# An attention phase with POOL summing the probabilities, two units in one product run, and the maxima of two heads in the two halves of the array

## What is computed

```python
o1 = attn(q, k1, v1, causal)            # branch 0: all keys, causal; values of rank 32
o2 = attn(q, ks, vs)                    # branch 1: 256 selected keys
o3 = attn(q, kw, vw, window of 64)      # branch 2: local window, causal
o = g[:, 0] * o1 + g[:, 1] * o2 + g[:, 2] * o3
return o @ Wproj                        # softmax over keys in each branch, scale 1/8
```

## Time and profile before

| | us |
|---|---|
| median of 3 runs | 2779.24 (2778.72 to 2779.59) |
| the profiled execution, its own time | 2781.34 |
| its span | 2779.4 |
| first and last product L1344 | 706.2 and 2379.5 |

### The profile page before, as it was taken

The page is one execution under the profiler, slowest core; times in us unless marked ns, Lnnn a source line. Parts: engine busy times, 40 slices in busy tenths (PEclk is TensorE's granted clock), DMA queues, the critical chain, the costliest instruction groups (busy, mean ns, idle before and its releaser), DMA issues. The chain is left out here.

```text
span 2779.4 us, 45396 instructions
## 1 busy us (share of the span) xinstructions
PE 2320.6 (83%) x16656; PEld 1545.5 (56%) x16656; DVE 1628.3 (59%) x3043; ACT 1266.2 (46%) x2777; POOL 669.8 (24%) x687
## 2 busy tenths in 40 slices
PE   5585858663999999999999999999999999601995
PEld 3464545442666666666666666566566666401884
DVE  4758575734466466466566576566565564450766
ACT  2354545440455555555455455555555555310442
POOL 0265656573011011011011011011010010145332
PEclk9697978765999999999999999999999999655997
DMA  2255555479547646556655565664664660611113
GB/s 97 97 219 184 216 187 201 172 269 226 126 93 146 132 101 139 122 118 131 127 121 122 120 136 114 136 129 104 137 137 96 138 130 10 158 39 47 48 53 110
DMA packets 222841, 360.53 MB, mean 130 GB/s; under 512 B 68794, under 2 KB 124701, under 8 KB 222240
## 3 DMA queue, kind: packets, MB, share of 16 engines
q1 hardware_dynamic: 216288, 348.43, 50.1%
q0 software_dynamic: 4320, 8.43, 0.9%
q10 hardware_dynamic: 2016, 0.77, 0.2%
HBM read 229.58 MB, written 126.56 MB: 128 GB/s over the span
## 5 line engine op out<-in xcount | busy, mean ns | idle before, releaser
L1370 ACT ACTIVATE prob<-ps 128x512 f32<-128x512 f32 (+5 forms) x1600 | 637.8, 441 | 665.8 <-PE ps L1325 656.3
L1434 DVE TENSOR_REDUCE maxima<-ps 128x1 f32<-128x512 f32 (+3 forms) x768 | 387.5, 547 | 291.4 <-PE ps L1250 147.0
L1344 PE MATMUL ps<-prob,plain 128*32 128x512 f32 (+5 forms) x3200 | 512.0, 443 | 0.0
L1400 POOL TENSOR_TENSOR products<-products,sums 128x256 f32<-128x256 f32 x192 | 140.8, 733 | 1540.3 <-DVE sums L1425 1539.0
L1439 DVE TENSOR_REDUCE maxima<-ps 128x2 f32<-128x512 f32 (+1 forms) x512 | 293.7, 606 | 192.6 <-PE ps L1261 98.4
L1425 DVE RECIPROCAL sums<-sums 128x256 f32<-128x256 f32 x192 | 331.9, 1736 | 97.6 <-ACT sums L1383 97.6
L1317 PE MATMUL ps<-q1a_s,k1a_s 128*128 128x512 f32 (+3 forms) x768 | 303.0, 395 | 0.0
L1325 PE MATMUL ps<-q1b_s,k1b_s 128*128 128x512 f32 (+3 forms) x768 | 301.1, 393 | 0.0
L1344 PE MATMUL ps<-prob,v_s 128*32 128x512 f32 (+3 forms) x1536 | 284.3, 491 | 0.0
L1250 PE MATMUL ps<-k1a_s,q1a_s 128*128 128x512 f32 (+3 forms) x768 | 234.5, 374 | 0.5 <-DVE maxima L1439 0.2
L1381 ACT ACTIVATE products<-ps,gates_a 64x512 f32<-64x512 f32 x192 | 131.0, 682 | 196.4 <-PE ps L1344 196.3
(11 more groups left out here) (333 smaller groups left out, 4889.8 us busy)
## 6 DMA issues: line engine op xcount, KB each, us to landing
qh_dram<-pairs SPq DMA_DIRECT2D x96, 512.0 KB, 2.7
kwh_dram<-pairs SPq DMA_DIRECT2D x64, 512.0 KB, 2.7
qa_s<-qh_dram SPq DMA_DIRECT2D x128, 256.0 KB, 4.7
kwa_s<-kwh_dram SPq DMA_DIRECT2D x128, 256.0 KB, 7.7
q1a_s<-qh_dram SPq DMA_DIRECT2D x128, 256.0 KB, 4.8
qb_s<-qh_dram SPq DMA_DIRECT2D x64, 256.0 KB, 9.3
kwb_s<-kwh_dram SPq DMA_DIRECT2D x64, 256.0 KB, 10.3
k1a_s<-k1ah_dram SPq DMA_DIRECT2D x32, 512.0 KB, 6.9
```

What stands on the lines that cost most here:

```text
L1344: mm = pe.matmul(ps[at:at + VD, SCORES + k % 2, q0 - c * CH:q0 - c * CH + w], w_, m.prob[:, n % PROBS, h, 0:w], start=first, stop=True, sk ...
L1370: act.activation(m.prob[:, u % PROBS, h, 0:w], ps[:, turn % SCORES, 0:w], ACT.Exp, scale=SCALE).then_inc(s["exp_done"], 1)
L1400: pool.tensor_tensor(o, o, m.sums[:, br, cc], ALU.mult).then_inc(s["divided"], 1)
L1434: ins = dve.tensor_reduce(partial[:, h, i, part:part + 1], bank[:, 0:w], AX, ALU.max)
```

## The change

- The products of branches 0 and 1 leave out the ones. Two units of the same width, one of branch 0's second half and one of a short list (branch 1, then branch 0's first half), are multiplied by their values in one run: two heads of each unit, in the four column tiles.
- POOL sums the probabilities of these 16 units into `acc`, in 12 additions and one copy a side. Two "total" steps a side multiply `acc` by the ones, in a fill bank; ACT copies them out ("take"). Branch 2 keeps its ones.
- The units stand in another order: the 9 of branch 2 first, then the 16 in pairs. `prob` holds 6 units.
- The queries are laid out so that the high parts of head 0 lie in partitions 0 to 63 and those of head 1 in 64 to 127. A maxima step takes both heads, each in 64 rows of the array (row tiles of 64 by 128), in two banks at once. There are 20 such steps a side, still with 3 fill banks and 40 reductions by DVE.
- `qb`, `kwb`, `ksb`, `vw` and `vs` are in one buffer instead of two, and have loads of their own, which wait until the side before has used them.
- The reciprocals and divisions of branch 0 stand at the beginning of the next side, both halves; those of branch 1 follow its total, in the last third of an odd side.

```diff
-SUMS = [(1, 0), (2, 0), (1, 1), (2, 1), (0, 0), (0, 1)]
-UNITS = units()
+def groups():
+
+
+    found = units()
+    sets = [found[2, c][i:i + 2] for c in range(NC) for i in range(0, len(found[2, c]), 2)]
+    short = found[1, 0] + found[1, 1] + found[0, 0]
+    return sets + [list(x) for x in zip(short, found[0, 1])]
+
+
+UNITS = sum(groups(), [])
+TOGETHER = [tuple(UNITS.index(x) for x in group) for group in groups()]
 LAST = [max(u for u, x in enumerate(UNITS) if x[:2] == k) for k in SUMS]
...
+OCCUPANTS = [-2, 0, 1, 2, 3, 1]
...
+def summing():
+
+
+    found, released, former = [], {}, {}
+    for u, (br, c, j, q0, w) in enumerate(UNITS):
+        if br == 2:
+            continue
+        if (br, c) not in former:
+            former[br, c] = u
+            continue
+        released[u] = len(found) + 1
+        if former[br, c] is not None:
+            released[former[br, c]] = len(found) + 1
+        found.append((u, br, c, former[br, c], q0 - c * CH, w))
+        former[br, c] = None
+    return found, released
+
+
+SUMMING, RELEASED = summing()
...
-PROBS = 4
+PROBS = 6
...
-    max0 = [("max0", side, h, i, part) for h in range(HP) for i in range(NT) for part in range(1 + (i >= NT // 2))]
-    max1, max2 = [[(kind, side, h, k) for h in range(HP) for k in range(NT // 2)] for kind in ("max1", "max2")]
-    todo = max2 + max1[:3] + [("rows", side, 2)] + max1[3:] + max0[:3] + [("rows", side, 1)] + max0[3:]
+    max0 = [("max0", side, i, part) for i in range(NT) for part in range(1 + (i >= NT // 2))]
+    max1, max2 = [[(kind, side, k) for k in range(NT // 2)] for kind in ("max1", "max2")]
+    todo = max2 + max1[:2] + [("rows", side, 2)] + max1[2:] + max0[:2] + [("rows", side, 1)] + max0[2:]
...
-    if w % 2 == 0 and w > 0:
-        pieces = [("divide", w - 1, len(SUMS) - 1, piece) for piece in range(PIECES)] + [("proj", w - 1, 1)]
+    if w > 0:
+        pieces = closing(w - 1)
-        ready = range(u - 2, u) if u >= 2 and u % 2 == 0 else range(u - 1, u) if u == len(UNITS) else ()
-        for done in ready:
-            todo.append(("products", w, done))
-        for done in ready:
-            if done in LAST:
-                k = LAST.index(done)
-                todo.append(("sum", w, k))
-                if w % 2 == 1 and (k < len(SUMS) - 1 or w == SIDES - 1):
-                    pieces += [("divide", w, k, piece) for piece in range(PIECES)]
-                    if SUMS[k][0] == 0:
-                        pieces.append(("proj", w, SUMS[k][1]))
+            todo += [("acc", w, op) for op, x in enumerate(SUMMING) if x[0] == u]
+        ready = [group for group, follower in zip(TOGETHER, TOGETHER[1:] + [(len(UNITS),)]) if follower[0] == u]
+        for group in ready:
+            todo.append(("products", w, group))
+            for done in sorted(LAST.index(x) for x in group if x in LAST):
+                todo.append(("sum", w, done))
+                if SUMS[done][0] == 2 and w % 2 == 1:
+                    pieces += [("divide", w, done, piece) for piece in range(PIECES)]
+                if SUMS[done] == (1, NC - 1):
+                    pieces += total_and_divide(w, 1)
         todo += pieces[:1]
         pieces = pieces[1:]
-    return todo + pieces
+    return todo + pieces + (closing(w) if w == SIDES - 1 else [])
+
+
+def total_and_divide(w, br):
+
+
+    pieces = [("total", w, br), ("take", w, br)]
+    for c in range(NC):
+        if w % 2 == 1:
+            pieces += [("divide", w, SUMS.index((br, c)), piece) for piece in range(PIECES)]
+            if br == 0:
+                pieces.append(("proj", w, c))
+    return pieces
+
...
             for side in range(1, SIDES):
+                units_done(side - 2, len(UNITS))
                 whole(side)
+                units_done(side - 1, WINDOWED)
+                window_exact(side)
+                if side + 1 < SIDES:
+                    window_keys(side + 1)
+                units_done(side - 1, LOCAL)
+                local_exact(side)
+                for br in (2, 1):
+                    row(side, br)
                 if side + 1 < SIDES:
                     local(side + 1)
-                for br in (2, 1, 0):
-                    row(side, br)
+                row(side, 0)
...
@@ -1240,81 +1339,103 @@
 
             def fill(n, kind, side, *a):
 
-                if n >= SPARES:
-                    pe.wait_ge(s["emptied"], n - SPARES + 1)
-                bank, k = ps[:, 8 - SPARES + n % SPARES, :], side % 2
+                def bank(h):
+                    if n + h >= SPARES:
+                        former = plan.fills[n + h - SPARES]
+                        if former[0] == "total":
+                            pe.wait_ge(s["taken"], plan.taken[former[1:]])
+                        else:
+                            pe.wait_ge(s["emptied"], plan.drained[n + h - SPARES])
+                    return ps[:, 8 - SPARES + (n + h) % SPARES, :]
+
+                k = side % 2
+                upper = [slice(HD * h, HD * h + HD) for h in range(HP)]
+                both = [bank(h) for h in range(plan.banks((kind,)))]
                 if kind == "max0":
-                    h, i, part = a
+                    i, part = a
                     once("far%d" % k, 16 * FAR * turn_no(side))
                     k0, k1 = part * CH, min((part + 1) * CH, (i + 1) * P)
-                    mm = pe.matmul(bank[:, 0:k1 - k0], m.q1a[:, k, h, i * P:(i + 1) * P],
-                                   m.k1a[:, k, k0:k1], start=True, stop=True)
+                    last = [pe.matmul(both[h][:, 0:k1 - k0], m.q1a[r, k, h, i * P:(i + 1) * P], m.k1a[r, k, k0:k1],
+                                      start=True, stop=True, skip_group_check=True) for h, r in enumerate(upper)]
                     if k1 == (i + 1) * P:
-                        mm = pe.matmul(bank[:, k1 - k0 - P:k1 - k0], m.ident_bf[:], m.causal_q[:],
-                                       start=False, stop=True, skip_group_check=True)
+                        last = [pe.matmul(both[h][:, k1 - k0 - P:k1 - k0], m.ident_bf[:], m.causal_q[:],
+                                          start=False, stop=True, skip_group_check=True) for h in range(HP)]
...
+                        t = 2 * a[0] + i
+                        for h, r in enumerate(upper):
+                            mm = pe.matmul(both[h][:, i * KEEP:(i + 1) * KEEP], m.qa[r, k, h, t * P:(t + 1) * P],
+                                           m.ksa[r, k, h, :], start=True, stop=True, skip_group_check=True)
...
+                elif kind == "total":
+                    pe.wait_ge(s["acc_done"], len(SUMMING) * side + max(n for n, x in enumerate(SUMMING) if x[1] == a[0]) + 1)
+                    for c in range(NC):
+                        for h in range(HP):
+                            at = c * NW + h * VD
+                            mm = pe.matmul(both[0][at:at + VD, :], m.plain[:], m.acc[:, a[0], c, h, :], start=True, stop=True,
+                                           skip_group_check=True)
...
+            def product(side, u, at, weights):
 
                 br, c, j, q0, w = UNITS[u]
-                n = side * len(UNITS) + u
-                k = side * len(SUMS) + SUMS.index((br, c))
-                first = u == 0 or u - 1 in LAST
-                pe.wait_ge(s["exp_done"], HP * (n + 1))
-                if first and k >= 2:
-                    pe.wait_ge(s["banks_free"], k - 1)
-                once("late%d" % (side % 2), 16 * LATE * turn_no(side))
-                for plain in range(2):
-                    for h in range(HP):
...
+            def products(side, group):
+
+                pe.wait_ge(s["exp_done"], HP * (side * len(UNITS) + group[-1] + 1))
+                for place, u in enumerate(group):
+                    br, c, j = UNITS[u][:3]
+                    if br == 0:
+                        once("late%d" % (side % 2), 16 * LATE * turn_no(side))
+                        values = [m.v1[:, side % 2, j, :]] * HP
+                    else:
+                        once("exact", 16 * EXACT * (side + 1))
+                        values = [(m.vs if br == 1 else m.vw)[:, j, h * VD:(h + 1) * VD] for h in range(HP)]
+                    if br == 2:
+                        product(side, u, 0, values)
+                        mm = product(side, u, NW, [m.plain[:]] * HP)
+                    else:
+                        mm = product(side, u, NW * place, values)
+                    mm.then_inc(s["products_done"], 1)
...
+                        old_side, old = divmod(u - PROBS, len(UNITS))
+                        if old in RELEASED:
+                            act.wait_ge(s["acc_done"], len(SUMMING) * old_side + RELEASED[old])
...
+                if kind == "take":
+                    br = step[2]
+                    n, rows = plan.fill_no["total", side, br], slice(NW * (side % 2), NW * (side % 2) + NW)
+                    act.wait_ge(s["fill_ready"], n + 1)
+                    for c in range(NC):
```

(27 more changed lines are left out.)

235 lines of the change are left out of this document (139 added, 96 removed).

## The result

The changed kernel takes 3027.28 us (median of 4 runs, 3025.96 to 3029.39) against 2779.41 for the kernel before on the same chip: ratio 1.0888, 95% interval 1.0869 to 1.0907. The forecast was 2805 with a range up to 2885. The direction was right; the loss was about nine times the one forecast.

A forecast was written before the change was run, and what follows sets the result against it. PE's matmuls were taken to bound the kernel (PE busy 83%). Terms -67 own work, +77 waits, +5 ends, +13 clock sum to +28 on 2781.3, less 2.1: 2807, stated as 2805; 8-in-10 range 2720 to 2885.

The forecast's parts named there:

- the clock: Behind the wait at an odd side's end, PE's clock halves for 3.4 us; 27 us in all, half taken: +13.
- the waits: New waits of PE at odd sides' ends, between double steps and before the projection, less earlier ones: +2.4 us a side, +77.
- waits at the seam: Around an odd side's end: 3.1 us for DVE before rows, 1.4 for POOL before total; 0.9 before the next projection.
- waits for the double steps: Three times a side two maxima steps follow each other and the second waits for a reduction: 0.9 us a side.
- PE's own work: PE's time in a side: products -3.9, maxima -4.0, changes of form +5.8; -2.1 us a side, -67 over 32.
- Rival (c): Product runs: units of one run go one behind another, so runs save half; 2895 us, chance 0.05.
- (a): Faster: many changes of form hide and reciprocals cost 1 us a side; 2680, with half of this 2740; chance 0.32.
- (b): Maxima: the two row tiles' weights load one behind the other, +2.5 us a side, +80; 2885 us, chance 0.13.
- FORMS: The experiments' rival theory: row tiles and changes of form between array tilings cost most of the loss; no chance given.
- Beginning and end: Last side closes both halves of branch 0 at the very end: +5 us; loads ahead of the first side: 0.
- DMA, 0: SP's DMAs rise from 32 to 40 a side; taken as 0, bound 3 us a side late.
- rival (d): Loads: the rows of the maxima or the queries land late, up to 2 us a side; 2870 us, chance 0.07.

The follow-up runs named there:

- tiles_later: Changed kernel, row tiles and double steps kept, seam reordered with branch 0's total, divisions and projections two units later still than in late_tiles: 2837.74 us, 1.0206.
- quarter_recip: Changed kernel inverting only the first 64 of each 256 denominators, the rest left out: 2906.57 us, 1.0442.
- before_early: Kernel before, with an odd side's last two divisions and projection issued all at once behind the next side's first unit: 2889.45 us, 1.0377.
- single_late: Changed kernel with whole-array maxima in single steps, branch 1's last two reciprocals behind the rows, branch 0's total and projections three units later: 2747.2 us, 0.9869.
- single_later: As single_late, whole-array maxima in single steps, but with the later order of tiles_later: 2719.35 us, 0.9776.
- late_tiles: Changed kernel, row tiles and double steps kept, branch 1's last two reciprocals behind the rows, branch 0's total and projections three units later: 2892.94 us, 1.0392.
- late_whole: As late_tiles, but with maxima over 128 rows of the whole array, still in double steps: 2856.54 us, 1.026.

## Why the forecast was wrong

Two steps of the forecast failed. The first and larger is the clock, one stretch of 3.4 us an odd side at half its chance, +13. The second is the waits, +77, in them the double steps of the maxima above all. The trace splits the loss. These are the thirty sides from the second `whole` to the last, of the kernel before and of the changed one:

```profile
750.40:2334.60 1584.20, 1550.03 (x12874) 980.59 (x12870) 972.59 (x1531) 826.03 (x1860) 175.93 (x240) 1.00 0.58 122
750.80:2566.70 1815.90, 1617.16 (x11433) 914.89 (x11433) 976.09 (x1532) 823.38 (x1860) 832.22 (x631) 0.90 0.47 107
```

They are 232 us longer. Of the changed kernel's time 352 us are at half clock, with 313 us of busy PE in them; the half of that, 156 us, is an estimate of the clock's price. PE's idle time, span less busy time, rose from 34 to 199 us, and what is left is PE's own work. The forecast's terms, scaled to thirty sides, beside what the trace has:

| | forecast, us | measured, us |
|---|---|---|
| waits at the seam | 81 | 87 |
| waits for the double steps | 27 | 82 |
| other waits, for ACT | 0 | 29 |
| less the waits of before | -36 | -34 |
| the clock | 12 | 156, estimate |
| PE's own work | -63 | -89 |
| sum | 21 | 231 |

Taken back one by one, the changes give: order of the seam 189.5 us (3027.28 to 2837.74), row tiles 14.5 (to 2823.23), double steps 103.9 (to 2719.35), and what is left of the change is 62.4 faster than before (2781.78). The shares depend on the order in which they are taken back. With the tiles first it is row tiles 70.4 (to 2956.93), double steps 69.2 (to 2887.77), order of the seam 168.4, because with the waits still there the tiles had a longer low clock behind them. The three together are 308 either way.

**PE's own work, -67: right as a sum, in part by luck.** At full clock two sides have 50.78 + 47.57 = 98.35 us of busy PE in tiles_later, where the kernel before had 103.32 in 105.6 us, from `whole` to `whole`: 2.5 a side less, against 2.1 forecast. The same with whole-array maxima is 97.91, so the products and totals save 2.7 a side where 3.3 was forecast, and the row tiles with their changes of form cost 0.2 where 1.2 was forecast. Rival (c), runs that save only half, is out. So is (a), which had PE's work at -4.3 a side and the waits smaller than forecast.

**Row tiles, rivals (b) and FORMS: not by themselves.** Both heads' matmuls run together: in tiles_later they start 0.004 us apart at most and end within 0.05 of each other, mostly 0.004, which rules out (b). The changes of form eat what that saves. Two heads of 512 columns (start, us):

```profile
1227.96 0.36 PE L1446 MATMUL ps<-q1b_s,k1b_s 128*128 128x256 f32 x1
1228.26 0.51 PE L1358 MATMUL ps<-k1a_s,q1a_s 64*128 64x512 f32 x2
1228.69 0.85 PE L1457 MATMUL ps<-prob,v_s 128*32 128x384 f32 x8
```

The pair ends 0.45 us behind the row before it; two whole matmuls take 0.46. The forecast had 0.41 for the pair, and 0.2 more where a whole matmul follows. What the tiles did cost in the changed kernel is low clock behind waits that were there anyway.

**"Other waits", 0.9 us a side for the double steps: the wait that was mis-sized most.** It had three places a side where two double steps follow each other, at 0.3 us each, 29 us in all. In the changed kernel PE sat idle for DVE ahead of L1358 and L1371 81.7 us in thirty sides, 2.7 a side, and taking the double steps away gave 69 us or 104, by the order. Three banks hold one double step and a half, so a step waits for a reduction of the one before also where scores stand between the two, and where a reciprocal is ahead of that reduction on DVE, it waits long:

```profile
1251.91 1.75 DVE L1599 RECIPROCAL sums<-sums 128x256 f32<-128x256 f32 x1 [0.41 <-ACT sums L1524]
1253.58 1.22 DVE L1614 TENSOR_REDUCE maxima<-ps 128x2 f32<-128x512 f32 x2
```

This is the 1.66 us before L1371 at 1254.95. With single steps DVE may be two reductions behind when a step begins, with double steps only one. The Trainium skill bears on this in "TensorEngine Tiling (Array Packing)", PSUM Bottleneck and Gotcha 1: tiling speeds the matmuls and not the emptying of PSUM, and row tiles write to different banks. The trace agrees that the banks count, and with whole-array maxima too: PE was idle 5.0 us of an odd side with two banks a step (52.50 less 47.48) and 1.9 with one (49.10 less 47.24).

**The waits at the seam, +4.5 an odd side and 0.9 for the projection: mechanism right, the sum by luck.** Before `rows` 1.67 us for DVE (forecast 3.1), before the total 1.95 for POOL (1.4), 2.7 once the clock held, before the projection 2.2 (0.9), and that before the second one, where the forecast had put it before the first. Together they are 5.8 us where 5.4 was forecast; one by one they are off by 0.6 to 1.4. DVE's last eight reductions with their reciprocals took 11.1 us (forecast 11.5), but PE had 9.6 us of work and short waits beside them where 8.4 was taken. What these waits bring behind them is the larger part. Waits for ACT, none over 0.6 us, are 29 us more, and the forecast had none.

**The clock, +13: the step that failed most.** It had one fall of 3.4 us an odd side, taken at half its chance: 0.8 us a pair of sides. Measured: 14 to 27 us of half clock in two sides, 20 or more in nearly all, in thirty sides 156 us by the estimate above. The step took its length from one wait in another phase, with nothing to show that a wait in this phase would be answered alike, and it put one fall where three waits stand. Why the low stretch is so long stays open.

**Beginning and end, +5: 13.3 and 6.5.** **DMA, 0: right**, and rival (d) is out. **POOL's own time, 0: right** but for the tail, which is next in line behind DVE: quarter_recip's 4.88 us.

Even sides were to be shorter than odd ones by 4 us. Counted from `whole` to `whole` the even ones are the longer, by 9 us, for the waits for the total and the projection stand at their head and the low clock behind them.

## What to carry to other kernels

Where PE is the bound, count a wait of PE at its length and the half clock that may follow: before_early paid 7.1 us for 4.1 of added idle time. Work moved to DVE, ACT or POOL costs nothing only if its consumer on PE has enough other work ahead of it; that is a matter of order, and 170 to 190 us here hung on a list of steps. A step that takes two of three buffers makes PE wait for reductions that it was ahead of before; a saving in matmul time must pay for that first. And a trial that fills waits with unread work must be charged with that work.

## What the runs showed of the hardware

- Idle time of PE of 1.36 to 2.2 us was followed by 1.2 GHz in some sides and not in others at the same place: the 1.66 us before L1371 in 7 of 15 odd sides of the changed kernel, and 1.36 to 1.41 us for ACT in 6 of 15 even sides of single_late. Gaps of 0.98 us were never followed by it in the sides of single_later.
- The low stretch was 3.4, 6.8, 10.2, 13.7, 17.1 or 20.5 us in the thirty sides. With nearly the same gaps it was longer with row tiles (late_tiles 143 us over the phase, late_whole 45). Why is not settled.
- Adding 24 matmuls of 512 columns that nobody reads, once in two sides, made the kernel 72 us faster.
- A pair of row tiles, 64 rows each and 512 columns, ended 0.45 us behind the matmul before it, about what two whole-array matmuls take (0.46).
